# Audio tower (patch embedding, attention, mixture of experts) on one core: q projected once and doubled, v's copy and z moved, another start and tail

## The reference

```python
# 1. patches of 8, 16 and 32 frames at half stride, projected: 127 + 63 + 31 = 221 tokens a batch
y_i = einsum('bnk,dk->bnd', patches_i(x), W_i) + b_i + pos_i + scale_emb[i]
h = concatenate([y_0, y_1, y_2], axis=1)                  # (16, 221, 128)
# 2. attention, 8 heads of 16
qkv = layernorm(h) @ w_qkv.T
h = h + softmax(q @ k.T / 4) @ v @ w_agg.T + b_agg
# 3. experts: the first 1024 tokens, two of eight experts each (the indices come as an input)
h[token] += sum over the two experts of weight * (gelu(z2 @ w1[e]) @ w2[e]),  z2 = layernorm(h)
```

## Time and profile before

| | |
|---|---|
| timed runs | 272.76, 273.70, 274.27 us, median 273.7 |
| the profiled execution's own time | 275.58 us |
| its span | 274.1 us |
| mean granted TensorE clock | 0.986 of full speed |
| TensorE matmuls busy | 260.4 us (95%), weight loads 222.7 (81%) |
| VectorE, ScalarE, GpSimd busy | 208.2 (76%), 142.6 (52%), 119.8 (44%) |
| chain that ended last, by engine | PE 78%, VectorE 10%, DMA 5%, GpSimd 3% |

### The profile page before, as it was taken

One profiled execution on the slowest core, in us unless ns is written; L12 is line 12 of the kernel. 1 busy time (PEld: TensorE's weight loads), 2 busy tenths in 40 slices (PEclk: granted clock), 3 DMA queues, 4 the chain that ended last, 5 costly groups with the idle time before them and its releaser, 6 DMA issues.

```text
span 274.1 us, 7238 instructions
## 1 busy us (share of the span) xinstructions
PE 260.4 (95%) x2897; PEld 222.7 (81%) x2897; DVE 208.2 (76%) x450; ACT 142.6 (52%) x221; POOL 119.8 (44%) x182
## 2 busy tenths in 40 slices
PE   8999989999899999999978999999999999999982
PEld 8899978879797979797958878788888888887751
DVE  1498489979899878888853968787777777877664
ACT  3780333725252525161543768585858686859330
POOL 4000021203348473838571263838383847463223
PEclk9999999999999999999997999999999999999979
DMA  6999200099100000000021101111111110000244
GB/s 243 402 383 419 109 1 2 0 302 293 31 14 15 22 18 21 17 22 15 23 47 30 32 28 42 38 42 38 39 38 43 30 39 28 20 28 22 76 125 116
DMA packets 16391, 22.29 MB, mean 81 GB/s; under 512 B 2415, under 2 KB 10327, under 8 KB 16327
## 3 DMA queue, kind: packets, MB, share of 16 engines
q1 hardware_dynamic: 14215, 18.67, 21.0%
q0 software_dynamic: 1760, 2.60, 3.1%
q10 hardware_dynamic: 384, 0.57, 0.7%
HBM read 17.43 MB, written 5.95 MB: 85 GB/s over the span
## 4 chain that ended last, share of the span: by engine, by line
PE 78%; DVE 10%; DMA 5%; POOL 3%; issue 2%; ACT 1%; SPq 0%; DVEq 0%; POOLq 0%; ACTq 0%
PE s_ps L1224 13%; PE e_ps L1134 12%; PE s_ps L1134 9%; PE e_ps L1418 7%; PE m_ps L1338 7%; PE m_ps L1405 5%; PE m_ps L1209 5%; PE m_ps L1199 5%; DVE nmax L887 3%; PE e_ps L1405 3%; DMA g_sb<-y_rows 2%; PE m_ps L1368 2%; PE e_ps L1427 2%; PE m_ps L1188 1%; PE m_ps L1312 1%
## 5 line engine op out<-in xcount | busy, mean ns | idle before, releaser
L887 DVE TENSOR_REDUCE nmax<-s_ps 128x4 fp32r<-128x884 f32 (+1 forms) x60 | 61.8, 1071 | 15.4 <-PE s_ps L1224 15.3
L615 ACT ACTIVATE probs<-s_ps 128x888 f32<-128x888 f32 (+1 forms) x60 | 51.4, 909 | 24.3 <-PE s_ps L1224 24.3
L455 POOL TENSOR_TENSOR var_eps<-mv,eps_t 128x2 f32<-128x2 f32 x16 | 8.0, 499 | 70.2 <-DVE mv L846 70.2
L505 POOL DMA_INDIRECT y_rows<-y_sb,idx_u x23 | 23.1, 1006 | 27.4 <-PE s_ps L1224 24.7
L486 POOL DMA_INDIRECT z_slots<-z,slot_u x20 | 23.4, 1171 | 16.1 <-PE s_ps L1224 11.4
L1338 PE MATMUL m_ps<-probs,v_aug 128*32 128x221 f32 (+1 forms) x480 | 25.8, 353 | 0.0
L1418 PE MATMUL e_ps<-w_now,hidT 128*128 128x128 f32 x184 | 23.1, 275 | 0.0
L1418 PEld LDWEIGHTS e_ps<-w_now,hidT 128*128 128x128 f32 x184 | 22.4, 192 | 0.0
L901 DVE SCALAR_TENSOR_TENSOR q_lo<-q_lo,c_sb,m_ps 128x442 fp32r<-128x442 f32 x15 | 10.1, 675 | 16.0 <-PE m_ps L1312 16.0
L599 ACT COPY zT<-m_ps 128x221 f32<-128x221 f32 x16 | 5.5, 345 | 30.5 <-PE m_ps L1189 30.5
L1134 PE MATMUL e_ps<-x_hi,w_hi 128*128 128x252 f32 (+2 forms) x128 | 20.8, 295 | 0.1
(11 more groups left out here) (170 smaller groups left out, 607.9 us busy)
## 6 DMA issues: line engine op xcount, KB each, us to landing
w_raw<-wt SPq DMA_DIRECT2D x6, 512.0 KB, 9.7
x_raw<-x SPq DMA_DIRECT2D x6, 512.0 KB, 10.7
w_sb<-w SPq DMA_DIRECT2D x1, 2048.0 KB, 9.7
z_slots<-z SPq DMA_DIRECT2D x1, 1518.0 KB, 13.3
zs<-z_slots SPq DMA_DIRECT2D x7, 198.0 KB, 2.7
x_raw<-x SPq DMA_DIRECT2D x4, 256.0 KB, 5.0
out<-h SPq DMA_DIRECT2D x11, 64.0 KB
c_sb<-consts SPq DMA_DIRECT2D x1, 599.5 KB, 12.8
```

The costliest lines, as they stand in the source:

```text
L505: g.indirect_dma_start(y_dram, bass.IndirectOffsetOnAxis(ap=idx_u[:, at:at + 1], axis=0), y_sb[:, n % 2, i, :], None).then_inc(y_out[n % 2 ...
L615: s.activation(probs[0:n, blk, 2 * f:2 * f + 2].rearrange("p t u n -> p t (u n)"), s_ps[0:n, 2 * f:2 * f + 2, 0:2 * NE], ACT.Exp, scale=DH ...
L887: v.tensor_reduce(nmax[0:n, blk, 2 * f:2 * f + 2, DH:DH + 2], src, AX_X, ALU.max, negate=True).then_inc(max_ready, 1)
```

## The change

- **Start.** Unit 0 is made from split operands like the others, its taps in the order 0, 1, 4, 5, 2, 3, 6, 7; x is laid out and loaded by phase (frame modulo 4) over the whole time; the splits of w's first two parts stand with those of x. 13 products of zeros instead of 10.
- **q from batch 8 on** (`DOUBLED`). One product projects all eight heads once; VectorE's `q_double` makes the doubled rows by two shuffles within groups of 32 partitions into `q_d`; ScalarE copies the high part behind k's; VectorE makes the low part from `q_d`, behind both k's, and the statistics of batch c + 2 come behind that. v's copy is ScalarE's, behind the exps.
- **z from batch 10 on** (`LATE_Z`) is made between the two maxima of the next cycle; its transpose and zT's copy are moved behind the second block's scores and behind o's copy.
- **Cycle 6**: the last scatter stands before hb (`keep_h`). **Cycle 7**: the transposes of zs stand behind the second block's scores; h's transpose stands behind those of zs in all cycles with experts.
- **Tail.** The last round's y is evacuated tile by tile on ScalarE, its second product stands in the last cycle behind two score pairs; both combines are VectorE's, t = 1 first, and the loads and stores in that order; other banks for the pairs, exps into a buffer of their own (over w1), o's copy between the exps, P*V of the last batch before the aggregation of the one before, zeros in two portions.

The diff, cut to this:

```diff
-RAW = 3
-WT_ORDER = (2, 3, 4, 5, 6, 7, 0, 1)
-X_PARTS = (tuple((0, 0, 256 * m, 256 * m + 256, ph, ph + 2) for m in range(2) for ph in (0, 2))
-           + tuple((g, sub, 256 * m, 256 * m + 256, 0, PHASES)
-                   for g, sub in ((0, 1), (1, 0), (1, 1)) for m in range(2)))
+X_PARTS = (tuple((0, 0, ph, ph + 1) for ph in range(PHASES))
+           + tuple((g, sub, ph, ph + 2) for g, sub in ((0, 1), (1, 0), (1, 1)) for ph in (0, 2)))
...
-LAST_ZEROS = 6
...
-FIRSTS = (0, 1, 2, 0)
-SECOND = (1, 2, 0, 1)
+DOUBLED = 8
+LATE_Z = 10
+TWICE = tuple([DH * u + i % DH for i in range(32)] for u in range(2))
...
+FIRST_ZEROS = 13
+LAST_ZEROS = (3, 6)
...
+FIRSTS = (0, 2, 1, 0)
+SECOND = (2, 1, 0, 1)
...
+FIRST_TAPS = (0, 1, 4, 5, 2, 3, 6, 7)
 def steps_of(u):
     scale, g, pieces = UNITS[u]
-    products = (RAW,) if u == 0 else (0, 2, 1) if u == 1 else range(3)
-    return [(u, k, i, c) for i in range(len(pieces)) for k in products for c in range(PATCHES[scale])]
+    if u == 0:
+        return [(u, k, i, c) for k in range(3) for c in FIRST_TAPS for i in range(len(pieces))]
+    return [(u, k, i, c) for i in range(len(pieces)) for k in range(3) for c in range(PATCHES[scale])]
...
-                for t in range(2):
+                for t in (1, 0):
...
-                if c > FFN_B:
+                if FFN_B < c < BATCH - 1:
+                    store_h1(c - 1)
+                elif c == BATCH:
+                    store_h1(c - 2)
                     store_h1(c - 1)
...
+            def keep_h(b):
                 pool.wait_ge(z_ready, b * 2 + 2)
...
+                if n == ROUNDS - 1:
+                    pool.wait_ge(y_last, i + 1)
+                elif i == 0:
+                    pool.wait_ge(y_ready, n + 1)
                 if i == 0:
-                    pool.wait_ge(y_ready, n + 1)
                     pool.wait_ge(idx_ready, n + 1)
...
                 if c + 2 < BATCH:
                     stage1(c + 2)
+                if b == FFN_B - 1:
+                    second_scores(c, 1)
+                    scatter(b, 1, 1)
+                if c + 2 < BATCH:
+                    keep_h(c + 2)
                 if n >= 0:
                     fetch_w1(n + 1, 2, ROUND)
                 if 0 < n <= ROUNDS and paced:
                     second_scores(c, 1)
                 scatter_y(n - 1, 2)
-                if 0 <= b < FFN_B:
+                if 0 <= b < FFN_B - 1:
                     second_scores(c, 1)
-                    scatter(b, 1, 1 if b == FFN_B - 1 else 0)
+                    scatter(b, 1, 0)
...
             def q_high(b):
-                act.wait_ge(q_done, b + 1)
-                s.copy(q_hi[:, b % 2, :, 0:N],
-                       m_ps[:, 0, 0:2 * N].rearrange("p (u n) -> p u n", u=2)).then_inc(q_hi_ready, 1)
+                if b >= DOUBLED:
+                    act.wait_ge(q_d_ready, 2 * (b - DOUBLED) + 2)
+                else:
+                    act.wait_ge(q_done, b + 1)
+                s.copy(q_hi[:, b % 2, :, 0:N], q_src(b)).then_inc(q_hi_ready, 1)
...
+            def late_v_copy(b):
                 act.wait_ge(v_done, b + 1)
...
+            def last_y(i):
+                n, at = ROUNDS - 1, TILES_BEFORE[ROUNDS - 1] + i
+                act.wait_ge(y_last_done, i + 1)
+                if i == 0:
+                    act.wait_ge(y_out[n % 2], 16 * sum(ROUND_TILES[n % 2:n:2]))
+                    act.wait_ge(slot_w_ready, n + 1)
+                s.activation(y_sb[:, n % 2, i, :], e_ps[:, i * P:(i + 1) * P], ACT.Copy,
+                             scale=slot_w[:, at:at + 1]).then_inc(y_last, 1)
             def last_exps(b):
+                act.wait_ge(w1_ready, N_TILES)
                 for i, (banks, f, blk) in enumerate(zip(SECOND, (0, 0, 1, 1), (0, 1, 0, 1))):
                     n = TILE_N[blk]
+                    if i == 2:
+                        o_raw_copy(b - 1)
                     act.wait_ge(s2_done, 2 * b + i + 1)
-                    s.activation(probs[0:n, blk, 2 * f:2 * f + 2].rearrange("p t u n -> p t (u n)"),
+                    s.activation(last_probs[0:n, blk, 2 * f:2 * f + 2].rearrange("p t u n -> p t (u n)"),
                                  pair_of(banks)[0:n, :, 0:2 * NE], ACT.Exp, scale=DH ** -0.5).then_inc(probs_ready, 1)
...
+            hi_w(0)
             hi_x(0)
             hi_x(1)
+            hi_w(1)
...
                     half_nmaxT_copy(c)
-                    o_raw_copy(c - 1)
                     last_exps(c)
                     continue
-                if 0 <= c + 1 < BATCH:
+                if 0 <= c + 1 < LATE_Z:
                     zT_copy(c + 1)
                 if n == 0:
...
                 if c - 1 >= 0 and n != 0:
                     o_raw_copy(c - 1)
+                if LATE_Z <= c + 1 < BATCH:
+                    zT_copy(c + 1)
...
-                if 0 <= c + 1 < BATCH:
+                if 0 <= c + 1 < DOUBLED:
...
                 if 0 <= c + 1 < BATCH:
                     k_high(c + 1)
+                if DOUBLED <= c + 1 < BATCH:
+                    q_high(c + 1)
+                if n == ROUNDS - 1:
+                    last_y(0)
                 if 0 <= c < BATCH:
                     exps(c, 1)
-                if c == BATCH - 2:
-                    last_v_copy(c + 1)
+                if DOUBLED <= c + 1 < BATCH:
+                    late_v_copy(c + 1)
+                if n == ROUNDS - 1:
+                    last_y(1)
...
+            def q_double(b):
+                dve.wait_ge(q_done, b + 1)
+                for u in range(2):
+                    v.stream_shuffle(q_d[:, u, :], m_ps[:, 0, 0:N], TWICE[u]).then_inc(q_d_ready, 1)
             def q_low(b):
                 dve.wait_ge(q_hi_ready, b + 1)
-                v.tensor_tensor(q_lo[:, b % 2, :, 0:N], m_ps[:, 0, 0:2 * N].rearrange("p (u n) -> p u n", u=2),
-                                q_hi[:, b % 2, :, 0:N].bitcast(F32), ALU.subtract).then_inc(q_ready, 1)
+                v.tensor_tensor(q_lo[:, b % 2, :, 0:N], q_src(b), q_hi[:, b % 2, :, 0:N].bitcast(F32), ALU.subtract).then_inc(q_ready, 1)
             def k_unit(b):
...
+            def combine(t, k):
+                dve.wait_ge(y_in[t], 16 * (len(SPANS[t]) + 1))
                 if k:
-                    dve.wait_ge(combined[0], 1)
-                v.tensor_tensor(h1k[:, :, 0, :], h1k[:, :, 0, :], g_sb[:, 0:FFN_B, k, :], ALU.add).then_inc(combined[0], 1)
+                    dve.wait_ge(combined[t], (1, 2)[t])
+                g = g_sb[:, FFN_B * t:FFN_B * (t + 1)]
+                if t == 0:
+                    v.tensor_tensor(h1k[:, :, 0, :], h1k[:, :, 0, :], g[:, :, k, :], ALU.add).then_inc(combined[0], 1)
+                else:
+                    for n, lo, hi in ((N1, 0, FFN_B - 1), (ffn_rows(FFN_B - 1, 1), FFN_B - 1, FFN_B)):
+                        v.tensor_tensor(h1k[0:n, lo:hi, 1, :], h1k[0:n, lo:hi, 1, :], g[0:n, lo:hi, k, :],
+                                        ALU.add).then_inc(combined[1], 1)
...
+            lo_x(0)
+            lo_x(1)
+            lo_w(0)
+            lo_w(1)
+            lo_x(2)
+            lo_x(3)
             lo_w(2)
...
                     ffn_z(c - 2)
                 if n == 0:
                     zsT_evac(0)
+                if c + 1 >= LATE_Z and c + 1 < BATCH:
+                    ln_z(c + 1)
                 if 0 <= c < BATCH - 1:
                     maxima(c, 1)
                 if c == BATCH:
                     nmaxT_copy(c)
                 elif c >= 0:
                     take_max(c)
+                doubled = DOUBLED <= c + 1 < BATCH
+                if doubled:
+                    q_double(c + 1)
                 if c - 1 >= 0:
                     turn(c - 1)
...
                     norm(c - 1)
-                if 0 <= c + 1 < BATCH:
+                if 0 <= c + 1 < BATCH and not doubled:
                     q_low(c + 1)
-                if c + 2 < BATCH:
+                if c + 2 < BATCH and not doubled:
                     ln_stats(c + 2)
                 if c == 0:
                     route_slots()
                 if 0 <= c + 1 < BATCH:
                     k_unit(c + 1)
                     k_low(c + 1)
-                if c + 2 < BATCH:
+                if doubled:
+                    q_low(c + 1)
+                    if c + 2 < BATCH:
+                        ln_stats(c + 2)
+                if c + 2 < min(LATE_Z, BATCH):
                     ln_z(c + 2)
...
-                if 0 < c + 1 < BATCH - 1:
+                if 0 < c + 1 < DOUBLED:
                     v_copy(c + 1)
...
                 if c == BATCH - 1:
-                    combine(0)
-                    combine(1)
+                    for t in (1, 0):
+                        combine(t, 0)
+                        combine(t, 1)
                 if c - 1 >= 0:
                     residual(c - 1)
-                if n == ROUNDS - 1:
-                    y_evac(n)
...
-                for u in range(2):
```

(54 more changed lines are left out.)

104 lines of the change are left out of this document (39 added, 65 removed).

## The result

The changed kernel takes **272.23 us** (median of 11 runs, nine of them at 271.89 to 272.63), the kernel before 273.43 on the same chip: a ratio of 0.9961, 95% interval 0.9943 to 0.9979. The forecast was 270.9, so the sign and the range (268.5 to 273.8) held, and the size did not. The profiled execution of the changed kernel took 272.13 (span 270.6), 3.45 less than the profiled one of before; the forecast for that difference was 2.8. That looks as if it had come out well, and it is where this case has most to teach: neither the size of the whole nor that of most terms was right.

The account below looks back on a forecast made before the run. TensorE, busy 95% of the span, was taken as the bound. Start +0.75, cycles 7 and 8 -2.0, cycles 9 to 13 -0.35, tail -1.2 sum to -2.8 us: 270.9 us from a 273.7 median, range 268.5 to 273.8.

Parts of the forecast that it names:

- cycle 7, z(6) to k(8): First cycle with experts: earlier scatter removes zs's wait, 1.4 us, and the half clock behind it, 2; 3.4 us sooner.
- Profile to median: Whole kernel: the 2.8 us summed on the profiled execution (275.58) applied unchanged to the timed median 273.7, giving 270.9.
- Start, plus 0.75: Unit 0: split products wait for ScalarE's splits, ending at 13.65 instead of 12.90; all 0.75 us is passed on.
- Cycle 8, gives back 1.4: Cycle 8: z of batch 9 comes late behind q's low part, TensorE waits 1.2 us; net for cycles 7 and 8 minus 2.0.
- Cycles 9 to 13, minus 0.35: Cycles 9 to 13: without q's second product, k's product still waits for h's copy; 0.07 us gained per cycle.
- A: Rival, cycles 8 to 14: TensorE the only bound, h's copy not late; 0.40 more for six cycles, 268.5; chance 0.12.
- Tail, minus 1.2: Last cycle: 0.1 from y's loads, 1.0 from ending the collision at o's product, 0.1 from the last store alone.
- About 0.4 us sooner: Tail: y's last tile scattered about 0.4 us sooner, as ScalarE evacuates the tiles one by one.
- the combine of t=1 lies before that landing, the other one behind it, as now: Tail: VectorE combines t=1 (1.75 us) before t=0 of y lands, and t=0 (1.76 us) after.
- B: Rival: clock falls again at the start or cycle 8's wait; 1.7 or 1.4 more, 272.5, both 274.0; chance 0.22.
- C: Rival, cycles 9 to 14: GpSimd and VectorE collide, 1 us per cycle, 276.9; chance 0.13.
- D: Rival, cycle 7: zs still late as a scatter lands late, so its 3.4 us stay; 274.3; chance 0.06.

Follow-up runs that it names:

- cycle 7's edit: Kernel before with only the last scatter ahead of hb on GpSimd and zs's transposes behind the second block's scores: 271.38 us, ratio 0.9938.
- before again: The kernel before, unchanged, run and profiled a second time: 273.16 us, ratio 1.0003.
- `LATE_Z = 9`: Changed kernel with z of batch 9, too, made between the maxima: 271.36 us, ratio 0.9934 against the kernel before.
- the undoubled kernel: Changed kernel with q projected by two products and copied as before for all batches: 271.21 us, ratio 0.9929 against the kernel before.
- the last cycle alone: Kernel before with only the change's last cycle (y's last tiles, loads and combines t=1 first, zeros, later P*V): 273.34 us, ratio 1.0015.
- The run with the product moved: Changed kernel with y's last product put ahead of the last cycle's first scores: 271.02 us, ratio 0.9935 against the kernel before.
- the start alone: Kernel before with only unit 0 from split operands, x laid out by tap phase and 13 zero products: 274.70 us, ratio 1.0039.
- the last two kernels: Changed kernel with z of batch 9 between maxima, y's products earlier, zsT's copy ahead of o's transpose: 268.49 us with q undoubled, 268.03 doubled (zsT's copy before shuffles).

## Why the prediction was off, step by step

The forecast's terms beside the same stretches of the changed kernel, less those of the kernel before in its second profile (the typical one) and in its first (the one summed over):

| | forecast | against the second | against the first |
|---|---|---|---|
| start, to z(6) | +0.75 | -0.20 | -0.79 |
| cycle 7, z(6) to k(8) | -3.4 | -1.50 | -3.03 |
| cycle 8, k(8) to k(9) | +1.4 | +0.75 | +0.74 |
| cycles 9 to 13, k(9) to k(14) | -0.35 | -0.40 | -0.33 |
| cycle 14, k(14) to k(15) | none | -0.16 | -0.17 |
| tail, k(15) to the end | -1.2 | +0.2 | +0.1 |
| sum | -2.8 | -1.3 | -3.5 |

- **Profile to median** ("the same difference gives 270.9"). This is the step that fails first. The working took 2.0 us for half clock in cycle 7 as if every execution paid it. One in five executions of the kernel before had a clock that low. The two profiles also size it, at 1.53 (40.27 and 38.74 from z(6) to k(8), with the same wait). Against the typical one, cycle 7's edit is worth the wait alone: 37.24 instead of 38.74, minus 1.5. The median of that edit by itself is 1.7 under the 273.07 of executions that kept the clock, and 2.0 under all. Its seven executions have none over 271.99, though clocks down to 0.984 still occur; its profile has half clock in the last cycle and the shorter tail all the same (23.95), so there it is not on the path. The 0.2 between 1.5 and 1.7 is within what the tail varies by.
- **Start, plus 0.75.** Units 0 to 2 together take no longer. Unit 1 begins at 13.27, against 12.32 and 12.90 in the two profiles of before, but the weight loads of a pass of 32 products of unit 2 take 3.78 us, not 4.00, with x laid out by tap phase, and h of batch 0 is transposed at 31.26 against 31.14 (before again). By z(6) it is minus 0.2, or minus 0.47 on average over the twelve profiles with the new start (110.92) and four with the old (111.39). So unit 0 does end later, by 0.37 and 0.95 (forecast 0.75), but it isn't passed on, and what was left out is what comes behind it: a pass of 32 products of unit 2 takes 3.88 us instead of 4.11. The change of layout is in the diff; I costed only the splits. The rows, first before again, then after:

```profile
17.95 4.00 PEld L1134 LDWEIGHTS s_ps<-x_hi,w_hi 128*128 128x128 f32 x32
18.06 4.11 PE L1134 MATMUL s_ps<-x_hi,w_hi 128*128 128x248 f32 x32
31.14 0.33 PE L1180 MATMUL m_ps<-c_sb,hT 128*128 128x128 f32 x1
```

```profile
13.27 2.02 PE L1184 MATMUL s_ps<-x_hi,w_hi 128*128 128x252 f32 x16
18.73 3.78 PEld L1184 LDWEIGHTS s_ps<-x_hi,w_hi 128*128 128x128 f32 x32
18.84 3.88 PE L1184 MATMUL s_ps<-x_hi,w_hi 128*128 128x248 f32 x32
31.26 0.33 PE L1226 MATMUL m_ps<-c_sb,hT 128*128 128x128 f32 x1
```

- **Cycle 8, gives back 1.4.** The mechanism was right (z of batch 9 behind q's low part) and its size half of the forecast one: 0.77 of wait for 1.2, 0.75 from k(8) to k(9) for 1.4. `LATE_Z = 9` takes all of it away.
- **Cycles 9 to 13, minus 0.35.** Measured minus 0.40, right by luck, as the reason was half wrong. That ScalarE's gelu, table load and h's copy set the pace was right, and so A fell. But the 0.07 a cycle stays with q undoubled; it comes from the reordering that the undoubled kernel keeps (z between maxima, h's transposes behind zs's, zT's copy), which of its parts I did not separate.
- **Tail, minus 1.2.** Measured plus 0.2, and 0.0 in the medians of the last cycle alone. The collision did go, the second o product (1.25 in the earlier trace rows) takes 0.27:

```profile
264.99 0.28 DVE L991 TENSOR_TENSOR o_sb<-o_tok,rden 128x112 f32<-128x112 f32 x1
...
265.86 0.27 DVE L991 TENSOR_TENSOR o_sb<-o_tok,rden 128x112 f32<-128x112 f32 x1
```

  Two steps failed. "About 0.4 us sooner" for y's last tile: counted from k(15), its scatter is at 7.12 us instead of 6.52, as its product stands behind two score pairs. And "the combine of t=1 lies before that landing, the other one behind it, as now": this took VectorE to be free when y lands, as it was before (1.92 of wait in the earlier trace rows). In the changed kernel the copy of the last maxima, behind the same product, is at 12.24 us after k(15) instead of 11.03, VectorE comes to the first combine at 14.79 with y there, and runs both in a row, t=0's at 16.55 instead of 15.16. Those 1.4 us eat the 1.0. The load hardly matters then. t=0's large load is issued fourth and lands 16.3 us after k(15) (262.14 against 245.81 in the profile with GpSimd's combine, whose loads are the same), 0.2 before VectorE gets to it. The run with the product moved has the chain back at 11.06 and gains 1.2. Full clock in the last PV gave nothing, as forecast.
- **Rivals.** A: k's product does wait for h's copy, and the cycle is 13.94 with the product of q or without. B: no half clock at the start or at cycle 8's wait in any profile here, though once in the new last cycle. C: refuted as priced. A copy of 128x3 took 0.50 in the median where it took 0.15 before, beside GpSimd's copies, and the cycle did not grow; at the combines the collision is 0.9 us. D: refuted, zs is in time.

The forecast's two errors of sign, start and tail, nearly cancelled between the first profile and the changed one (minus 1.5 and plus 1.3), which is luck, and is why the profiles' difference looked right. Between medians the half clock had no such counterweight.

Of the rules weighed: by the Trainium skill ("TensorE: Matmul & The Clock Gate", section on why this matters for your kernels) a gap as short as these is harmless. The second profile of before agrees (1.61 us of wait, clock 1.00) and the first does not (1.54, then 0.52): a row at half clock is a thing that happens in some executions, and is priced by their share. The estimate of 0.26 us for a shuffle, scaled from the tier table of "VectorE: DVE Perf Modes" of the Trainium skill, was low: it takes 0.41, as the transpose that I took as nearest row.

**Open** are why the clock falls in one execution and not in another with the same wait, and once without a wait; why zs took 4.0 us to land in the profile of the start alone; and what sets the 13.65 us of the last two kernels' cycle.

## What to carry to other kernels

Before a profile's durations are summed, compare its span and mean granted clock with those of many executions: a stretch at half clock is worth its time only as often as it happens. An instruction taken off the busiest engine gains nothing where that engine waits at the next instruction for another; look for that wait first (here 0.6 us behind a table load) and fill it with work that stood behind it. Here that was worth 0.28 us a cycle, and taking the work out as well gained nothing more. When a tail hangs on a store and a reload, count from one landmark to the last store's issue in both versions, and to the time at which the engine that uses the data is free.

## What the hardware showed beyond that

The same 32 fp32r products of unit 2 take 3.88 us with x, their moving operand, laid out by tap phase (weight loads 3.78), and 4.11 (4.00) with two phases interleaved; unit 1's passes of 16 hardly differ, 2.02 and 2.01. A shuffle of 221 fp32 columns out of PSUM takes 0.41 us on VectorE and its mask load 0.01. A GpSimd add of 93x512 beside VectorE's add of 128x640 makes two of the latter take 2.63 us in place of 1.74. The granted clock fell to 0.50 in one last cycle behind 5 us in which TensorE shows no idle time.
